# Moving the last layernorm's sums into the down-projection's evictions, and its normalisation from VectorE to ScalarE

## What is computed

```
x = x + _layernorm(attn(_layernorm(x)))
# _L0_ffn_ref, on _layernorm(x):
gated = silu(gate) * up                            # 2048 -> 8192
return einsum('bsh,dh->bsd', gated, w_down)        # 8192 -> 2048
x = x + _layernorm(_L0_ffn_ref(...))

def _layernorm(x, axis=-1, eps=1e-5):
    m = mean(x); v = var(x)
    return (x - m) / sqrt(v + eps)
```

## Time and profile before

| | us |
|---|---|
| median of two runs (2804.55, 2804.85) | 2804.7 |
| the profiled execution | 2802.73 |
| its span, first to last instruction, slowest core (6) | 2801.2 |
| spans of the eight cores | 2792.4 to 2801.2 |
| TensorE busy (matmuls) | 2393.3 |
| VectorE busy | 647.0 |
| ScalarE busy | 565.8 |
| mean granted TensorE clock | 0.94 |

### The profile page before, as it was taken

How to read it: one execution, slowest core, us unless ns; L and a number is a source line. 1 busy time by engine, 2 the same in 40 slices (tenths; PEclk the granted TensorE clock), 3 DMA queues, 4 the chain that set the end, 5 groups by cost and what they waited for, 6 DMA issues and landing times.

```text
span 2801.2 us, 26790 instructions; the slowest of 8 cores (2792.4 to 2801.2 us)
## 1 busy us (share of the span) xinstructions
PE 2393.3 (85%) x10912; PEld 1060.2 (38%) x10912; DVE 647.0 (23%) x672; ACT 565.8 (20%) x621; POOL 157.7 (6%) x269
## 2 busy tenths in 40 slices
PE   1998788888778888687799999999999999999960
PEld 1443333333333333233444444444444444444420
DVE  5501333333332333466400000000000000000022
ACT  5513333333333333222000000000000000000011
POOL 0000000000000000000000000000000000111000
PEclk9999889998998998898899999999999999999985
DMA  6541100110100100723444444444444545545488
GB/s 188 133 94 23 23 16 15 21 18 16 23 16 16 23 16 1 120 91 105 75 76 76 75 76 77 78 79 76 76 76 75 83 60 75 76 68 76 75 127 151
DMA packets 67622, 186.33 MB, mean 67 GB/s; under 512 B 4912, under 2 KB 37680, under 8 KB 62256
## 3 DMA queue, kind: packets, MB, share of 16 engines
q0 software_dynamic: 64048, 159.47, 34.3%
q1 hardware_dynamic: 3456, 25.17, 3.0%
HBM read 302.12 MB, written 25.17 MB: 117 GB/s over the span
## 4 chain that ended last, share of the span: by engine, by line
PE 77%; DVE 9%; DMA 4%; issue 4%; ACT 3%; another core or an unknown queue 2%; ACTq 0%; DVEq 0%; POOL 0%; POOLq 0%
PE ps L352 18%; PE ps L651 16%; PE ps L663 16%; PE ps L710 15%; PE ps L305 4%; PE ps L446 4%; DVE afp L523 4%; PE ps L424 3%; ACT abf L433 2%; DMA x2s<-afp 2%; DVE afp L192 1%; DMA out<-afp 1%; DVE abf L396 1%; DVE afp L580 1%
## 5 line engine op out<-in xcount | busy, mean ns | idle before, releaser
L352 PE MATMUL ps<-abf 128*128 128x512 bf16 x2048 | 516.7, 417 | 54.7 <-DVE afp L523 53.4
L710 PE MATMUL ps<-abf 128*128 128x512 bf16 x2048 | 448.4, 382 | 13.1 <-DVE abf L722 8.2
L651 PE MATMUL ps<-abf 128*128 128x512 bf16 x2048 | 454.2, 380 | 2.6 <-DVE abf L631 2.6
L663 PE MATMUL ps<-abf 128*128 128x512 bf16 x2048 | 452.5, 379 | 0.0
L352 PEld LDWEIGHTS ps<-abf 128*128 128x128 bf16 x2048 | 215.6, 106 | 351.0 <-issue 152.4
L433 ACT ACTIVATE abf<-ps,afp 128x1024 bf16<-128x1024 f32 x256 | 270.3, 1111 | 166.7 <-PE ps L446 103.6
L710 PEld LDWEIGHTS ps<-abf 128*128 128x128 bf16 x2048 | 201.0, 98 | 260.5 <-issue 23.7
L651 PEld LDWEIGHTS ps<-abf 128*128 128x128 bf16 x2048 | 201.0, 98 | 245.2 <-issue 5.0
L663 PEld LDWEIGHTS ps<-abf 128*128 128x128 bf16 x2048 | 200.2, 98 | 241.8
L679 DVE TENSOR_TENSOR abf<-afp,ps 128x1024 bf16<-128x1024 f32 x64 | 78.2, 1222 | 809.3 <-PE ps L663 809.3
L424 PE MATMUL ps<-abf 128*128 128x512 bf16 x512 | 148.5, 386 | 125.0 <-ACT abf L433 105.9
(11 more groups left out here) (61 smaller groups left out, 946.9 us busy)
## 6 DMA issues: line engine op xcount, KB each, us to landing
abf<-wg POOLq DMA_DIRECT2D x64, 512.0 KB, 5.1
abf<-wu POOLq DMA_DIRECT2D x64, 512.0 KB, 5.1
abf<-wd POOLq DMA_DIRECT2D x64, 512.0 KB, 5.5
afp<-xb SPq DMA_DIRECT2D x24, 1024.0 KB, 6.3
abf<-wq POOLq DMA_DIRECT2D x16, 512.0 KB, 7.3
abf<-wk POOLq DMA_DIRECT2D x16, 512.0 KB, 5.6
abf<-wv POOLq DMA_DIRECT2D x16, 512.0 KB, 5.3
abf<-wo POOLq DMA_DIRECT2D x4, 2048.0 KB, 34.5
```

What stands on the lines that cost most here:

```text
L352: op("t", lambda e, slot=slot, kc=kc, g=g, bank=bank: e.matmul(Pv(bank * 512, [(1, 512)]), Bv(W3 + slot * 2048 + kc * 128, [(1, 128)]), Bv ...
L651: op("t", lambda e, slot=slot_g, kc=kc, half=half, gb=gb: e.matmul(Pv(gb * 512 + half * 512, [(1, 512)]), Bv(W3 + slot * 2048 + kc * 128, ...
L663: op("t", lambda e, slot=slot_u, kc=kc, half=half, ub=ub: e.matmul(Pv(ub * 512 + half * 512, [(1, 512)]), Bv(W3 + slot * 2048 + kc * 128, ...
L710: op("t", lambda e, hc=hc, qc=qc, i=i, base=base, j=j: e.matmul(Pv(qc * 512, [(1, 512)]), Bv(GMAP[hc] + qc * 128, [(1, 128)]), Bv(base + i ...
```

## The change

In stage F, each quarter's evictions are followed by the statistics of that quarter. ScalarE, for its four row blocks, waits for its own last instruction, then runs `Square` over the 512 features just written with a sum as second output, waits again, and runs `Identity` with a sum. VectorE, for its four, runs a `reduce_sum` over 512 features and, after a wait for its own instruction, a `scalar_tensor_tensor` (x * 1.0 * x) with a sum. The sums go to two tables of 8 x 4 numbers beside the statistics. All of these raise `sFe` and `vFe`, which now count 12 a quarter instead of 4, and TensorE's wait at the start of a quarter is for all 12.

In stage G, `ln_site` is gone. VectorE adds the four partial sums of each row block (six small additions), works out mean and variance, and after ScalarE's square root the reciprocal and `-mean * rstd`. The normalised rows are written by ScalarE (`Identity` with scale and bias from SBUF) instead of by VectorE.

```diff
@@ TensorE, start of a quarter
             if qd == 0 and j >= 1:
-                w("t", sFe, 4 * j)
-                w("t", vFe, 4 * j)
+                w("t", sFe, 12 * j)
+                w("t", vFe, 12 * j)
@@ ScalarE, behind its four evictions of each quarter
+        for qc in range(4):
+            w("s", sFe, sFe.n)
+            op("s", lambda e, qc=qc, j=j: e.activation(
+                Fv(XS0, [(1, 512)]),
+                Bv(OFM + qc * 2048 + j * 512, [(1, 512)]),
+                AF.Square, accum_out=Fv(ST + 96 + qc * 4 + j, [(1, 1)])), (sFe, 1))
+            w("s", sFe, sFe.n)
+            op("s", lambda e, qc=qc, j=j: e.activation(
+                Fv(XS0, [(1, 512)]),
+                Bv(OFM + qc * 2048 + j * 512, [(1, 512)]),
+                AF.Identity, accum_out=Fv(ST + 64 + qc * 4 + j, [(1, 1)])), (sFe, 1))
@@ VectorE, behind its four evictions of each quarter
+        w("v", vFe, vFe.n)
+        for qc in range(4, 8):
+            op("v", lambda e, qc=qc, j=j: e.reduce_sum(
+                Fv(ST + 64 + qc * 4 + j, [(1, 1)]),
+                Bv(OFM + qc * 2048 + j * 512, [(1, 512)]), axis=AX.X), (vFe, 1))
+            w("v", vFe, vFe.n)
+            def sq(e, qc=qc, j=j):
+                return e.scalar_tensor_tensor(
+                    Fv(XS1, [(1, 512)]),
+                    Bv(OFM + qc * 2048 + j * 512, [(1, 512)]),
+                    1.0,
+                    Bv(OFM + qc * 2048 + j * 512, [(1, 512)]),
+                    ALU.mult, ALU.mult,
+                    accum_out=Fv(ST + 96 + qc * 4 + j, [(1, 1)]))
+            op("v", sq, (vFe, 1))
@@ stage G, each row block
-        par, M, RS = ln_site(
-            src_v=fr_v, src_s=fr_v,
-            dump=lambda: Bv(WDA, [(1, 2048)]),
-            vwaits=vw, swaits=sw)
+        par = qc % 4
+        SM, SQ2, M, M2, VE, SD, RS, MR = 0, 1, 2, 3, 4, 5, 6, 7
...
+        w("v", vI, vI.n)
+        op("v", lambda e, par=par, qc=qc: e.tensor_tensor(
+            stat(par, SM), Fv(ST + 64 + qc * 4, [(1, 1)]),
+            Fv(ST + 64 + qc * 4 + 1, [(1, 1)]), ALU.add), (vI, 1))
...
+        op("s", lambda e, par=par: e.activation(
+            stat(par, SD), stat(par, VE), AF.Sqrt,
+            bias=Fv(ST + 40, [(1, 1)])), (sSd, 1))
+        w("v", sSd, sSd.n)
+        op("v", lambda e, par=par: e.reciprocal(stat(par, RS), stat(par, SD)), (vI, 1))
+        w("v", vI, vI.n)
+        op("v", lambda e, par=par: e.tensor_scalar(
+            stat(par, MR), stat(par, M),
+            stat(par, RS), -1.0, ALU.mult, ALU.mult), (vI, 1))
         slot = qc % 3
-        w("v", vI, vI.n)
+        w("s", vI, vI.n)
         if qc >= 3:
-            w("v", dAC[slot], 16 * (qc // 3))
-        op("v", lambda e, qc=qc, slot=slot, par=par, M=M, RS=RS: e.tensor_scalar(
+            w("s", dAC[slot], 16 * (qc // 3))
+        op("s", lambda e, qc=qc, slot=slot, par=par: e.activation(
             Fv(slot * 2048, [(1, 2048)]),
             Bv(OFM + qc * 2048, [(1, 2048)]),
-            stat(par, M), stat(par, RS), ALU.subtract, ALU.mult), (vG, 1))
+            AF.Identity, bias=stat(par, MR), scale=stat(par, RS)), (vG, 1))
```

More of the change, by code:

```diff
@@ new lines, in build_nc @@
+        SM, SQ2, M, M2, VE, SD, RS, MR = 0, 1, 2, 3, 4, 5, 6, 7
+        if qc == 0:
+            w("v", sFe, 48)
+            w("v", vFe, 48)
+            w("v", tF, 64)
+            w("s", sFe, 48)
+            w("s", vFe, 48)
+            w("s", tF, 64)
+        w("v", vI, vI.n)
+        op("v", lambda e, par=par, qc=qc: e.tensor_tensor(
+            stat(par, SM), Fv(ST + 64 + qc * 4, [(1, 1)]),
+            Fv(ST + 64 + qc * 4 + 1, [(1, 1)]), ALU.add), (vI, 1))
+        op("v", lambda e, par=par, qc=qc: e.tensor_tensor(
+            stat(par, M2), Fv(ST + 64 + qc * 4 + 2, [(1, 1)]),
+            Fv(ST + 64 + qc * 4 + 3, [(1, 1)]), ALU.add), (vI, 1))
@@ new lines, in build_nc @@
+        w("v", vI, vI.n)
+        op("v", lambda e, par=par: e.tensor_tensor(
+            stat(par, SM), stat(par, SM), stat(par, M2), ALU.add), (vI, 1))
+        op("v", lambda e, par=par, qc=qc: e.tensor_tensor(
+            stat(par, SQ2), Fv(ST + 96 + qc * 4, [(1, 1)]),
+            Fv(ST + 96 + qc * 4 + 1, [(1, 1)]), ALU.add), (vI, 1))
+        w("v", vI, vI.n)
+        op("v", lambda e, par=par, qc=qc: e.tensor_tensor(
+            stat(par, M2), Fv(ST + 96 + qc * 4 + 2, [(1, 1)]),
+            Fv(ST + 96 + qc * 4 + 3, [(1, 1)]), ALU.add), (vI, 1))
@@ new lines, in build_nc @@
+        w("v", vI, vI.n)
+        op("v", lambda e, par=par: e.tensor_tensor(
+            stat(par, SQ2), stat(par, SQ2), stat(par, M2), ALU.add), (vI, 1))
+        w("v", vI, vI.n)
+        op("v", lambda e, par=par: e.tensor_scalar(
+            stat(par, M), stat(par, SM), 1.0 / D, None, ALU.mult), (vI, 1))
+        w("v", vI, vI.n)
+        op("v", lambda e, par=par: e.tensor_scalar(
+            stat(par, M2), stat(par, M), stat(par, M), None, ALU.mult), (vI, 1))
+        w("v", vI, vI.n)
@@ new lines, in build_nc @@
+        op("v", lambda e, par=par: e.scalar_tensor_tensor(
+            stat(par, VE), stat(par, SQ2), 1.0 / D, stat(par, M2),
+            ALU.mult, ALU.subtract), (vI, 1))
+        w("s", vI, vI.n)
[4 more added lines that the diff above has]
+        op("v", lambda e, par=par: e.reciprocal(stat(par, RS), stat(par, SD)), (vI, 1))
+        w("v", vI, vI.n)
+        op("v", lambda e, par=par: e.tensor_scalar(
+            stat(par, MR), stat(par, M),
+            stat(par, RS), -1.0, ALU.mult, ALU.mult), (vI, 1))
@@ L766, in build_nc @@
     assert tD.n == 8 and vD.n == 8 and tE.n == 128 and vGa.n == 64
-    assert tF.n == 64 and sFe.n == 16 and vFe.n == 16 and vG.n == 8
+    assert tF.n == 64 and sFe.n == 48 and vFe.n == 48 and vG.n == 8
     assert tTR.n == 16 and vA.n == 16 and vXA.n == 16 and tT3.n == 8 and vA3.n == 8
```

## The result

The changed kernel takes 2824.67 us (median of 11 runs), the kernel before 2804.7 (median of 10): the ratio is 1.0073, with a 95% interval of 1.0062 to 1.0084. That is +20 us, where the prediction said +20.7.

A forecast was written before the change was run, and what follows sets the result against it. The prediction took TensorE to bound stage F and DMAs the tail. Boundaries 19.0, clock 1.5 and slot turnaround 0.2 gave +20.7 us on 2804.7, i.e. 2825.4 us, range 2817 to 2834.

The forecast's parts named there:

- Who bounds: Stage F is bound by TensorE; the tail, 94 us after the last matmul, by DMAs: copy, then accumulation.
- ScalarE's pieces: Stage F quarter ends: eight added pieces of 0.82 us behind 2.06 us of evictions, ending after 8.7 us (7.3 to 10.2).
- VectorE's pieces: Stage F quarter ends: four row blocks of 1.56 us behind 2.48 us of evictions, ending after 8.8 us (8.5 to 9.2).
- +6.3 us a boundary: TensorE waits 8.8 us instead of 2.48 at each of three stage F boundaries: +19.0 us (14.4 to 23.1).
- The clock: Slow matmuls after longer idle at stage F's boundaries: 0.5 us extra each (0 to 1.0), +1.5 us.
- The tail: Fourth quarter and new stage G: hidden by the copy, 18 us of cover, worth 0.
- The slot turnaround: Stage G: output between accumulating DMAs takes 2.09 us on ScalarE instead of 1.35; taken as +0.2 us (0 to 1.5).
- Payback by the weight stream: Rival, stage F: loads use TensorE's boundary waits, so later weight waits shrink; 2804.7 us, chance 0.02.
- A shorter tail: Rival, stage G: VectorE paces it, tiles fall from 5.15 to 3.1 us, -10 us net; 2815 us, chance 0.03.
- Table loads: Rival, stage F: ScalarE reloads its table between Square, Identity and Copy, +31 us; 2856 us, chance 0.03.
- The statistics didn't overlap: Rival, stage F boundaries: statistics overlap evictions, so stalls are about 2 us or less; 2812 us, chance 0.04.
- the clock didn't stay low: Rival, stage F: after 9 us idle the slow stretch costs 6 us more a quarter, +18; 2843 us, chance 0.03.

The follow-up runs named there:

- free: Changed kernel, but the statistics raise semaphores of their own and TensorE waits for the evictions alone; 2804.8 us, ratio 0.9989 to the kernel before.
- gold: Changed kernel's stage F with the kernel before's stage G (full sums over 2048, output on VectorE); 2825.6 us, ratio 1.0075 to the kernel before.
- nowait: Changed kernel without an engine's waits for its own last statistic, each throw-away result having its own place; 2821.1 us, ratio 1.0065 to the kernel before.
- double: Changed kernel with every stage F statistic worked out twice and TensorE waiting for both; 2846.5 us, ratio 1.0148 to the kernel before.
- best2: Changed kernel, TensorE not waiting for statistics, residual loaded into SBUF during stage F, all row blocks' statistics finished at once, plain stores; 2766.0 us, ratio 0.9843.
- best2_late: best2 without statistics in stage F: whole sums of 2048 and squares behind the last quarter; 2775.6 us, ratio 0.9875 to the kernel before.

## Why the prediction was right

**Who bounds.** Confirmed by free and gold: stage F is bound by TensorE, all of the +20 us stands there, and the tail is the DMAs'. The tail's length is 94.4 us in both profiles, equal within the scatter of 3 us between cores.

**ScalarE's pieces.** Forecast 0.72 us for the pair and 0.10 for the wait, 0.82 from start to start; measured 0.72 (2358.96 to 2359.68), 0.09 and 0.81. The end of the group was forecast 8.7 us after the quarter and came at 8.6. That the same 0.1 us also cost an overlap was hidden in the 1.98 us of the row that the price was taken from, so it did no harm to the sum; nowait shows it. It did harm the lower bound: that took 0.66 us for a pair without a wait, with 0.06 of overlap, and nowait shows 0.61.

**VectorE's pieces.** Sum 0.68, product 0.69 as forecast. The accumulator's read was forecast at 0.09, between the bounds 0 and 0.18, and is 0.08. A row block is 1.40 us, not 1.56: the read starts 0.07 us before the product's end, and the next sum starts together with the read, so that neither adds to the path. VectorE's group ended 0.5 us earlier than forecast (8.3 for 8.8). It released TensorE only where it had begun later, at the second boundary. That ScalarE ended last, while the sum was built on VectorE's 8.8, moved the boundary by 0.2 us and no more: the two ends lay so close together that one of them coming too early cost the forecast little.

**TensorE.** Forecast +6.3 us a boundary, +19.0; measured +6.2, 26.7 - 8.2 = +18.5. The lower bound was wrong: 14.4 let ScalarE end at 7.3 us and forgot VectorE, for which the prediction's own lower bound is 8.5, so that (8.5 - 2.5) x 3 = 18.0 is the least that its terms allow. nowait shows the effect, where ScalarE alone would have released TensorE earlier and VectorE held it.

**The clock.** Forecast +1.5 us. From the restart to the fast weight loads it now takes 4.2, 4.3 and 5.5 us, before 3.3, 3.4 and a stretch of 3.2 that began 1.3 us after the restart. At half the pace these 4.1 us more are worth 2.0. Stage F as a whole is 20.5 us longer, of which 18.5 are boundaries, 0.6 weights and so 1.4 the rest. The size came out right, but in part by luck: the stretches vary by more than 1 us for the same idle time (see the last section).

**The tail.** Forecast 0 for stage G, with the first tile 15.2 us after the last matmul and others every 3.1; measured 15.5 and 3.0. The slot turnaround was given 0.2 and is 0 within what the tails show. The output took the forecast 2.09 us.

**The rivals.** Payback by the weight stream: weights are waited for 0.6 us more, not less, and the double run shows a full price. A shorter tail: not here, and with the copy removed it was longer by 7.9. Table loads: one load stands in stages F and G, at L798, none among Copy, Square and Identity. The statistics didn't overlap, and the clock didn't stay low. For a time beyond 2% the prediction wanted two of these rivals together and gave it 0.03, as much as to each alone, which was too much.

**The sum.** In the two spans the terms are 18.5 for the boundaries, 1.4 for the clock and small things, 0.6 for weights (not forecast, and less than the scatter between cores), 0 for the tail, and 0.7 less ahead of stage F (within the scatter, too): 19.8 us, where 20.7 was forecast.

## What to carry to other kernels

Work that is "hidden behind the matmuls" is hidden only if no matmul waits for its semaphore: put a count of its own on it, and let TensorE wait for the evictions alone; here that is the difference between +20 us and 0. Before work is moved off a tail, ask which wait ends last there; outputs every 3.0 us instead of every 5.15 were worth nothing behind a copy that landed 20 us after the third of them was ready in the kernel before. Once the copy and the accumulating DMAs were gone the same partial sums were worth 12 us of tail and 9.6 us of time, and the version with both (best2) is 1.4 to 1.6% faster than the kernel before.

## What the runs showed of the hardware

- A wait of an engine for its own last instruction cost 0.19 to 0.20 us on ScalarE and VectorE: 0.1 as a visible gap and 0.1 as a lost overlap (row blocks of 1.21, 1.40 and 1.60 us with none, one and two waits). With a throw-away output of its own for each instruction such a wait isn't needed.
- A VectorE instruction with a sum as second output is followed by a record of its own, 0.08 us (ScalarE's is 0.19), and the next VectorE instruction starts beside it (2360.81 in the timeline after).
- The slow stretch behind an idle TensorE (granted clock at the lower level, 1.2 GHz) doesn't grow in step with the idle time, and may be missing. After 9.4 us of idle in weight loads it ended 4.2, 4.3 and 5.5 us after the restart in the changed kernel and 4.2, 3.4 and 5.1 in gold, after 16.0 us in double 4.6, 4.3 and 5.8. After 3.20 us it ended at 3.3, 3.4 and 4.5 in the kernel before, and at the third boundary of free there was none (granted clock 1.00 from 2593 to 2597), as this row of its weight loads shows:

```profile
2593.21 54.95 PEld L712 LDWEIGHTS ps<-abf 128*128 128x128 bf16 x256 [3.20 <-issue]
```

- In best2's tail core 3 stored its 1 MB tiles with plain DMAs at 350 to 430 GB/s, and in best2_late's tail all eight cores stored at once at 340 to 360 GB/s each (2756 to 2760, DMA share 1.00 to 1.02). The accumulating DMAs ran at 156 GB/s, on all eight cores at 154 to 158, also at a share of 1.0.
- Loads beside a weight stream are not free at half-busy DMA engines: 8 MB in stage F cost TensorE 14 us of waits in pieces of 1 MB (17.1 against 3.3) and 17 in pieces of 256 KB (20.3) on the slowest cores; in the mean of eight cores it is 12 and 13.
